# First layer's sums in the build of a graph network: counts as the stationary operand instead of the features

## The reference

```python
out_deg = jnp.clip(jax.ops.segment_sum(ones, src, num_segments=n), 1.0)
in_deg  = jnp.clip(jax.ops.segment_sum(ones, dst, num_segments=n), 1.0)
h = label * (out_deg ** (-0.5))[:, None]
agg = jax.ops.segment_sum(h[src], dst, num_segments=n)
return agg * (in_deg ** (-0.5))[:, None]
```

## Time and profile before

| | us |
|---|---|
| median of 3 runs | 4291.0 |
| lowest and highest run | 4282.44, 4293.14 |
| the profiled execution | 4288.49 |
| its span, first to last instruction | 4286.6 |
| first and last start of L1719 (the windows of the build) | 278.0, 1210.3 |

### The profile page before, as it was taken

The page is one execution under the profiler, slowest core; times in us unless marked ns, Lnnn a source line. Parts: engine busy times, 40 slices in busy tenths (PEclk is TensorE's granted clock), DMA queues, the critical chain, the costliest instruction groups (busy, mean ns, idle before and its releaser), DMA issues. The chain is left out here.

```text
span 4286.6 us, 68644 instructions
## 1 busy us (share of the span) xinstructions
PE 3701.8 (86%) x20966; PEld 2089.1 (49%) x20967; DVE 3410.2 (80%) x5084; ACT 2868.1 (67%) x3215; POOL 515.0 (12%) x1356
## 2 busy tenths in 40 slices
PE   3569999999973999999969999998799999989998
PEld 3546766667651333333433333333233333369898
DVE  9998888988865999998599999987999999741222
ACT  2046767767653898999859999995799999810011
POOL 0025555555510000000000000000000000000000
PEclk9989999999986999999989999999899999999999
DMA  2023444544446444443334444431444444268899
GB/s 71 0 70 118 151 132 136 156 121 146 134 168 73 180 162 158 156 161 129 113 120 158 161 159 162 163 114 68 160 163 158 158 157 150 100 232 289 295 340 323
DMA packets 490425, 661.06 MB, mean 154 GB/s; under 512 B 147927, under 2 KB 463193, under 8 KB 490074
## 3 DMA queue, kind: packets, MB, share of 16 engines
q1 hardware_dynamic: 384664, 523.99, 36.9%
q10 hardware_dynamic: 105540, 134.07, 8.9%
HBM read 520.63 MB, written 137.34 MB: 153 GB/s over the span
## 5 line engine op out<-in xcount | busy, mean ns | idle before, releaser
L1932 PE MATMUL psum<-sb_arena 128*65 128x448 f32 x4116 | 1730.9, 543 | 187.6 <-DVE sb_arena L1448 174.7
L1448 DVE SCALAR_TENSOR_TENSOR sb_arena<-sb_arena 128x896 f32<-128x896 f32 x1029 | 1071.4, 1088 | 207.5 <-ACT sb_arena L2334 191.1
L2326 ACT ACTIVATE psum<-sb_arena,sb_sj 128x896 f32 (+1 forms) x1029 | 1041.0, 1012 | 215.0 <-PE psum L1910 95.3
L2334 ACT ACTIVATE sb_arena<-psum,sb_sj 128x896 f32<-128x896 f32 x1029 | 1020.9, 992 | 99.2 <-PE psum L1943 98.5
L1413 DVE CUSTOM_DVE_ANT_0 sb_arena<-sb_arena 128x6272 uint8<-128x6272 uint8 (+2 forms) x189 | 990.4, 5240 | 71.9 <-DMA sb_arena<-linked 31.4
L1932 PEld LDWEIGHTS psum<-sb_arena 128*65 128x65 f32 x4116 | 557.4, 138 | 880.5 <-issue 502.2
L966 DVE TENSOR_SCALAR sb_arena<-sb_arena 128x392 f16<-128x392 f16 x2352 | 652.2, 344 | 0.0
L1943 PE MATMUL psum<-sb_arena,sb_ones 128*128 128x448 bf16 x2058 | 567.3, 358 | 45.8 <-ACT sb_arena L2303 25.0
L2151 ACT ACTIVATE sb_arena<-psum 128x784 f16<-128x784 f32 x392 | 323.2, 824 | 281.3 <-PE psum L1719 278.2
L1719 PE MATMUL psum<-sb_arena 128*128 128x392 f16 x2352 | 470.7, 336 | 39.1 <-DVE sb_arena L966 29.0
L1943 PEld LDWEIGHTS psum<-sb_arena,sb_ones 128*128 128x128 bf16 x2058 | 185.8, 97 | 600.1 <-issue 392.2
(11 more groups left out here) (288 smaller groups left out, 1947.3 us busy)
## 6 DMA issues: line engine op xcount, KB each, us to landing
sb_arena<-counts SPq DMA_DIRECT2D x245, 896.0 KB, 6.3
sb_arena<-counts SPq DMA_DIRECT2D x245, 672.0 KB, 4.4
sb_arena<-linked SPq DMA_DIRECT2D x147, 784.0 KB, 7.0
counts<-sb_arena ACTq DMA_DIRECT2D x56, 1344.0 KB, 5.7
linked<-sb_arena ACTq DMA_DIRECT2D x60, 784.0 KB, 3.4
sb_arena<-records SPq DMA_DIRECT2D x784, 6.0 KB, 1.8
counts<-sb_arena ACTq DMA_DIRECT2D x1, 5488.0 KB, 19.9
records<-sb_arena SPq DMA_DIRECT2D x1, 3124.0 KB, 8.9
```

The source lines that it names most:

```text
L1448: nc.vector.scalar_tensor_tensor(YE[:, r % RING, :], YE[:, r % RING, :], 1.0, counts_of(g, j), ALU.min, ALU.mult).then_inc(p_ready, 1)
L1932: last = nc.tensor.matmul(psum[0:D + 1, t, 0:HALF], HF[:, r * (D + 1):(r + 1) * (D + 1)], YE[:, r % RING, t * HALF:(t + 1) * HALF], start= ...
L2326: nc.scalar.activation(stage_of(odd, r), of.rearrange("p (t d) -> p t d", t=2), ACT.Relu, bias=sj8[:, r:r + 1], scale=1.0 - SLOPE).then_in ...
L2334: nc.scalar.activation(YE[:, r % RING, :].rearrange("p (t d) -> p t d", t=2), stage_of(odd, r), ACT.Exp, bias=sj2[:, r:r + 1]).then_inc(e_ ...
```

## The change

The counts become the stationary operand. For each source block r the half's 448 targets are cut into blocks of 128, 128, 128 and 64 (`BLOCKS_OF`; in an odd half the 64 belong to the targets 0 to 63 and go to PSUM partitions 64 to 127), and each block moves all pieces and the ones together: `Lp`, 193 columns. The sums thus lie target by feature at once, four groups of 193 columns in banks 6 and 7. ScalarE moves both banks with one instruction and divides by the unit of the counts. VectorE adds the three pieces into `LAGG` behind the keys of window 5 (`pieces_added`, `ADD_AT`), which waits for `half_out`. `chunk_back`, `chunk_sums` and their semaphores are gone, and TensorE waits for `half_out` behind the turns of window 2.

```diff
-                def chunk_back():
-                    for b in range(CB):
-                        to = psum[:, 6, b * (D + 1):(b + 1) * (D + 1)]
-                        nc.tensor.matmul(to, LA[:, b * BLK:(b + 1) * BLK], fold[:], start=True, stop=False)
-                        last = nc.tensor.matmul(to, LB[0:D + 1, b * BLK:(b + 1) * BLK], unscale[:], start=False, stop=True)
-                    last.then_inc(chunk_turned, 1)
...
-                    if k == 0:
+                    if k == 2:
                         pe.wait_ge(half_out, h + 1)
-                        if slot == 0:
-                            chunk_back()
-                    if k == 2 and slot == 0:
-                        pe.wait_ge(chunk_out, c + 1)
                     if k >= 2:
                         for r in range(NB * (k - 2) // (WH - 2), NB * (k - 1) // (WH - 2)):
                             counts_r = stage[:, slot, r * HALF:(r + 1) * HALF]
-                            nc.tensor.matmul(psum[:, 6, 0:HALF], L12[:, r, :], counts_r, start=(r == 0), stop=(r == NB - 1))
-                            last = nc.tensor.matmul(psum[0:D + 1, 7, 0:HALF], L3p[:, r, :], counts_r, start=(r == 0), stop=(r == NB - 1))
+                            for i in range(4):
+                                n0, n1 = BLOCKS_OF[slot][i]
+                                p0 = slot * (BLK - n1 + n0)
+                                to = psum[p0:p0 + n1 - n0, 6 + i // 2, i % 2 * PW:(i % 2 + 1) * PW]
+                                last = nc.tensor.matmul(to, counts_r[:, n0:n1], Lp[:, r, :], start=(r == 0 and i % 2 == 0), stop=(r == NB - 1),
+                                                        skip_group_check=True)
...
-                    nc.scalar.copy(LA[:, odd * HALF:(odd + 1) * HALF], psum[:, 6, 0:HALF])
-                    nc.scalar.copy(LB[0:D + 1, odd * HALF:(odd + 1) * HALF], psum[0:D + 1, 7, 0:HALF]).then_inc(half_out, 1)
+                    nc.scalar.activation(LSUM[:, odd, :].rearrange("p (b n) -> p b n", b=2), psum[:, 6:8, 0:2 * PW], ACT.Copy, scale=1.0 / UNIT).then_inc(half_out, 1)
...
+                def pieces_added(odd, c, h):
+                    dve.wait_ge(half_out, h + 1)
+                    of = LSUM[:, odd, :].rearrange("p (a n) -> p a n", a=4)
+                    wide = CB * (D + 1)
+                    to = (LAGG[:, bass.ds(c * wide, wide)] if not isinstance(c, int) else LAGG[:, c * wide:(c + 1) * wide]).rearrange("p (a f) -> p a f", a=CB)
+                    p0 = odd * (BLK // 2)
+                    parts = ((0, BLK, 0, 3, 4 * odd, 4 * odd + 3), (p0, p0 + BLK // 2, 3, 4, 3, 4))
+                    for q0, q1, a0, a1, b0, b1 in parts:
+                        nc.vector.tensor_tensor(of[q0:q1, a0:a1, 0:D], of[q0:q1, a0:a1, 0:D], of[q0:q1, a0:a1, D:2 * D], ALU.add)
+                        nc.vector.tensor_copy(to[q0:q1, b0:b1, D], of[q0:q1, a0:a1, 3 * D])
+                    dve.drain()
+                    for q0, q1, a0, a1, b0, b1 in parts:
+                        nc.vector.tensor_tensor(to[q0:q1, b0:b1, 0:D], of[q0:q1, a0:a1, 0:D], of[q0:q1, a0:a1, 2 * D:3 * D], ALU.add)
```

More of the change, by code:

```diff
@@ L49 @@
 LAG = 4
+ADD_AT = 6
+BLOCKS_OF = (((0, 128), (128, 256), (256, 384), (384, 448)), ((64, 192), (192, 320), (320, 448), (0, 64)))
 RING = 7
@@ L168, in gnn_kernel @@
         sub_src = sub_src.rearrange("p (w b) t -> p w b t", w=SS)
[L170 to L173, removed]
+        PW = 3 * D + 1
+        Lp, o = view(o, [BLK, NB, PW], bf16)
+        L12, L3p = Lp[:, :, 0:2 * D], Lp[:, :, 2 * D:PW]
+        LSUM, o = view(o, [BLK, 2, 4 * PW], fp32)
         LAGG, o = view(o, [BLK, (CHUNKS + 1) * CB * (D + 1)], fp32)
@@ L290, in gnn_kernel @@
         half_out = sem("half_out")
-        chunk_turned = sem("chunk_turned")
-        chunk_out = sem("chunk_out")
         counts_stored = sem("counts_stored")
@@ new lines, in _ @@
+                with dve.Fori(0, CHUNKS) as c:
+                    for odd in range(2):
+                        h = c * 2 + odd
+                        for k in range(WH):
+                            s, at = k % WS, k % SS
+                            if k == ADD_AT:
+                                pieces_added(odd, c, h)
+                            dve.wait_ge(rel_ready, h * WH + (k + WS + 1))
+                            dve.wait_ge(turn_done, h * WH + (k + 1))
+                            nc.vector.tensor_tensor(sub_src[:, at], iota_t[:, :, 0:2 * ST],
+                                                    src_rel[:, s, :].unsqueeze(1).broadcast_to([BLK, BLK, 2 * ST]), ALU.is_equal)
+                            for t in range(2 * ST):
+                                last = nc.vector.tensor_scalar(sub_key[:, at, t, :], sub_iota[:, t // ST, :],
+                                                               rel[:, k, 3 * t:3 * t + 1], None, ALU.is_equal)
+                            last.then_inc(keys_ready, 1)
@@ L1013, in first_variance @@
                     dve.drain()
-                dve.wait_ge(chunk_out, CHUNKS)
+                dve.drain()
                 first_degrees(0, NB - CB)
@@ L1024, in _ @@
                 score_squares()
-                dve.wait_ge(chunk_out, CHUNKS + 1)
+                for odd in range(2):
+                    pieces_added(odd, CHUNKS, NH + odd)
+                dve.drain()
                 dve.wait_ge(root_out, 4)
@@ L2162, in _ @@
                                 store_piece(1 - odd, PIECE_AT.index(k), h)
-                            if k == 1 and odd == 1:
-                                chunk_sums(c)
                             if k % GRP == GRP - 1:
@@ L2178, in _ @@
                 root_of(4, 0, NB - CB)
-                chunk_sums(CHUNKS)
                 root_of(5, NB - CB, NB)
```

## The result

| | before | after |
|---|---|---|
| median of the runs | 4291.0 us | 4369.4 us (4366.8 to 4374.6, 4 runs) |
| ratio, with 95% interval | | 1.0185 [1.0173, 1.0197] |
| span of the profiled execution | 4286.6 us | 4367.9 us |
| an even half, an odd half (means over the loop, without the last odd one) | 62.7, 71.1 us | 71.4, 73.4 us |
| loop: from its first count matmul to the end of its last | 932.8 us | 1009.1 us |

The change is 1.85% slower, 78 us by the medians and 81 by the spans of the two profiles; forecast were 71 (4362, in a range of 4328 to 4392).

A forecast was written before the change was run, and what follows sets the result against it. TensorE was taken as the bound, with VectorE close behind. The terms +127 - 45 - 11 + 5 - 4 = +72 on the profiled 4288.5 gave 4360.5, so a median of 4362 us (1.7% slower), range 4328 to 4392.

The forecast's parts named there:

- sums, per block: TensorE's sums of one source block: 0.56 us against 0.375, so +0.185 us, bounds +0.14 and +0.24.
- sums in the loop, 686 blocks: The extra block price over the loop's 14 halves of 49 blocks: +127 us, bounds +96 and +165.
- `chunk_back`: Start of odd halves: its fp32 matmuls and the half clock behind them go, 7 x 6.4 = -45 us.
- wait for `half_out` and the move: Half starts: window 1's counts run during ScalarE's move, 0.8 us saved a half, -11 us in all.
- VectorE's additions: Adding the pieces costs VectorE 1.5 us a half, hidden under TensorE's longer half: 0.
- pass behind the loop: 49 dearer blocks there cost +9 us, about 4 vanish in TensorE's idle time: +5 us, bounds +2 and +9.
- end of the pass: From ScalarE's copy to the degrees, one move and additions replace two copies, chunk_back and a move: -4 us.
- The price of a block: Four products 0.333 us, two changes of shape at 0.095 each, 0.04 for exposed loads: 0.56 us a block.
- Rival A: Sums on TensorE: the 64-column product costs no change of shape, 0.333 us a block, 4200 us in all; 7%.
- rival B: Sums on TensorE: only one change of shape a block is paid, no difference overall, 4297 us; 4%.
- Rival C: Half starts: TensorE's clock falls, two windows at half clock, +28 us, 4390 in all; 11%.
- Rival D: VectorE's additions are not covered, costing 21 us, 4383 in all; 3%.

The follow-up runs named there:

- e9: The changed kernel with the last additions of each half on VectorE done four times instead of once; 4360.9 us, one run.
- e4: The changed kernel with TensorE waiting for half_out behind the turns of window 0 again, not window 2; 4377.9 us, one run.
- e1: The changed kernel with the fourth stationary block 128 wide instead of 64, for all but one block of a half; 4272.0 us, ratio to before 0.9968.
- e2: The changed kernel with the second block of a two-block window starting with its 64-column product, beside the first's; 4283.1 us, ratio to before 0.9991.
- e3: The kernel before with the second product of 47 of 49 blocks narrowed from 65 stationary columns to 64 (degrees too small); 4434.2 us, one run.
- e7: The kernel before with six of seven blocks of chunk_back's turning left out (output wrong); 4271.0 us, one run.
- e10: The kernel of e8 with two windows' record loads per half issued from ScalarE instead of three; 4262.4 us, ratio to before 0.9946.
- e8: The kernel of e1 with three of a half's 28 windows' record loads issued from ScalarE's queue instead of SyncE's; 4234.8 us, ratio to before 0.9883.
- e5: The kernel of e1 with one record load a window instead of two (part of the edges not counted); 4211.8 us, one run.

## Why the prediction was right, step by step

The form of the sum held, and the measured terms add up to what the two profiles show (81 us between their spans). By its own terms the forecast is 4360.5 + 2.5 = 4363; it says 4362.

| step | forecast | measured |
|---|---|---|
| sums, per block | +0.185 us | +0.195 |
| sums in the loop, 686 blocks | +127 | +134 |
| `chunk_back` | -45 | -45 |
| wait for `half_out` and the move | -11 | -13 (what is left) |
| VectorE's additions | 0 | about 0 (e9) |
| pass behind the loop | +5 | +4.5 |
| end of the pass | -4 | -4.3 |
| all that lies ahead of the loop and behind the pass | 0 | +5 |

How the measured column comes about: from window 4 to the end an even half took 62.28 - 9.3 = 53.0 us and now takes 70.93 - 9.0 = 61.9, 8.95 more for the 46 blocks in it: 0.195. 49 blocks are 9.55, but a whole even half grew only by 71.4 - 62.7 = 8.7, so 0.9 a half came back at its start, 14 x 0.9 = 13. That is a remainder, put down to the wait and the move; e4 supports it from the other side with 14.5. An odd half grew by 73.4 - 71.1 = 2.3 us, 6.4 less than an even one, and this is put down to `chunk_back`, on the assumption that the wait brought the same in both. 134 - 45 - 13 = 76 us is what the loop grew by (1009.1 - 932.8).

- **The price of a block.** The forecast's mechanism, both changes paid in every block, is shown by the starts at 808.90 and 809.11 and by e1, e2 and e3. Its size was 0.01 too low. The changes and loads cost 0.094 in and 0.12 out, and the second product behind a change starts 0.094 later, not 0.083: 0.22 in place of the 0.23 estimated. But the counts behind the sums lose 0.04 us a window too (1.21 against 1.17), 0.02 a block, which the forecast left out: 0.333 + 0.22 + 0.02 = 0.573, against 0.375. Rival A (no price, 7%) and rival B (one of the two paid, 4%) fall with the starts.
- **What the runs show of its terms.** The change into 64 columns that the forecast read at L1675 shows in two windows of the kernel before. Six counts take 604.82 - 603.81 = 1.01 us with the 128-column turns behind them, and 607.07 - 605.96 = 1.11 us with the 64-column L1675 behind them: 0.10 for the change. That the load behind a change is exposed for 0.02 us, or for 0 to 0.05 as in the bounds, no run shows as a term of its own. Change and load show together, 0.094 in and 0.12 out. The fp32 matmuls of the earlier trace rows show no price of a change of rows: L2001 (128 rows) starts at 3855.55 and again at 3856.00, 0.45 apart, and L2002 (2 rows) at 3856.47 and again at 3856.95, 0.48 apart; across the two changes it is 0.47 and 0.46. The forecast's size came out near the truth because the 64-column L1675 gives it. The rows of the kernel before, timeline of TensorE:

```profile
603.81 1.17 PE L1719 MATMUL psum<-sb_arena 128*128 128x392 f16 x6
604.82 0.55 PE L1693 MATMUL psum<-sb_ident,sb_arena 128*128 128x128 f16 x7
...
3855.55 0.61 PE L2001 MATMUL psum<-sb_arena,sb_W3c 128*128 128x448 f32 x1
...
3856.95 0.53 PE L2002 MATMUL psum<-sb_arena,sb_W3b 2*128 2x448 f32 x1
```

- **Rival C**, a lower clock at the half starts: some even halves do have a first window at half clock for most of its length (up to 2.70 us in place of 1.44), which makes their mean 71.4 instead of 70.9. That is 3 us in the whole, not 28.
- **Rival D** falls: VectorE is idle 11.9 us of a half in the changed kernel, and e9 shows the additions hidden. Their size was 1.9 us and not 1.5, which changes nothing while they are covered.
- **The rest of the kernel**, +5 us (0.9 ahead of the loop and 3.9 behind the pass): it holds no instruction of the change, and 3.9 is well inside the 15 us by which this part differs between the twelve traces. Its cause is open.

What the forecast missed did not touch its number, and that is luck: the change made the halves longer and not shorter. It wrote that any change in a block's price goes straight into the time, and named VectorE as the next bound ("VectorE follows closely"), with rival A at 4200. Had a block really cost 0.333 us, the kernel would have come not to 4200 but near e1's 4272: the next bound is SyncE's issuing, 66 us a half, a resource that the profile's busy shares do not list, because issuing is not counted as busy. It hides in the changed kernel, whose halves are 71 to 74 us. The forecast's -45 for `chunk_back` was right only for that reason; without the longer sums, most of it is lost to SyncE (7.4 us in e7's loop, where 38 were taken out).

## What to carry to other kernels

Before putting a stationary operand of 64 columns between full ones, count the changes of shape: here each lone narrow product cost 0.22 us, more than two and a half products of 193 columns, so padding it to 128 (e1) or setting two narrow ones side by side (e2) gave the better kernel. Before taking work off the bound, ask for the waits of the issuing queues too: SyncE's, without any wait in e1, e2, e7 and e10, was full at 1.18 to 1.24 us an issue, and of a gain below its 66 us a half most was lost where others wait for its loads (e7's loop kept 7.4 us of 38). Then move enough of its issues that it waits again (three of 28 windows in e8, where two in e10 were too few).

## What the runs showed that was not expected

- 65 stationary columns behave as 128, 64 do not: behind L1705 the 65-column L1706 starts after 0.19 us and the next L1705 0.18 later (607.68, 607.87, 608.05 before), with 64 columns it is 0.29 and 0.31, and one column fewer cost 149 us in e3.
- Two 64-column products side by side start 0.11 us apart and share the changes; in a window of two blocks this saved 0.25 us.
- SyncE needs 1.18 us an issue on the mean for loads of 6 KB (a value load and its unpacking for every second one included). In e1 its quickest windows of two issues take 1.97 us and the mean one 2.37; what holds the slower ones up was not followed. With one issue a window in place of two it waits 171 of 723 us (e5).
- With the late half starts of e1 the clock falls too: its TensorE spends 93 us of its loop at half clock, e5's 10.
- TensorE idles 1.3 to 3.8 us at the loop's end, once a chunk (1.26 at 741.60 in e3, 2.64 at 544.69 in e1, 3.77 at 411.20 in e7), for a reason that no run here isolates.
